# Weights first, four steps' inputs made on chip, the early convolution inside step 1, and another issuer for the stage stores

## The reference

```python
# x (B, T, D), cond (B, D)
# layer 0: depthwise causal convolution along T with K = 128 taps; cond is the tap matrix (tap, channel)
x = x + (conv_causal(x, cond[:, None, :]) + b)
# layer 1: a GRU over T, its first state is cond, then the residual
gi = x_t @ W_ih + b_ih ; gh = h @ W_hh + b_hh          # (B, 3D) each
r = sigmoid(i_r + h_r) ; z = sigmoid(i_z + h_z)
n = tanh(i_n + r * h_n) ; h = (1 - z) * n + z * h      # 64 steps, one after the other
out = x + all h
```

## Time and profile before

| | us |
|---|---|
| three runs, median | 1177.78 (1176.2 to 1178.16) |
| profiled execution, its own time | 1179.38 |
| its span | 1177.5 |
| TensorE busy | 1135.4 (96%) |
| VectorE busy | 690.0 (59%) |
| ScalarE busy | 506.3 (43%) |
| GpSimd busy | 145.7 (12%) |
| mean granted TensorE clock | 0.997 |

### The profile page before, as it was taken

One profiled execution on the slowest core, in us unless ns is written; L12 is line 12 of the kernel. 1 busy time (PEld: TensorE's weight loads), 2 busy tenths in 40 slices (PEclk: granted clock), 3 DMA queues, 4 the chain that ended last, 5 costly groups with the idle time before them and its releaser, 6 DMA issues.

```text
span 1177.5 us, 16672 instructions
## 1 busy us (share of the span) xinstructions
PE 1135.4 (96%) x5796; PEld 960.1 (82%) x5796; DVE 690.0 (59%) x1026; ACT 506.3 (43%) x965; POOL 145.7 (12%) x175
## 2 busy tenths in 40 slices
PE   1999999999999999999999999999999999999997
PEld 1977887878888888888888888888888888888885
DVE  2746775766775375555555655655555555655554
ACT  4527776767775343333323233333333333233332
POOL 0320010001001421111111000111111111100110
PEclk9999999999999999999999999999999999999999
DMA  9988888888863601110111111011111011111001
GB/s 247 286 193 167 160 172 165 173 174 171 174 151 91 147 18 37 36 35 25 31 36 36 36 36 28 25 36 36 36 36 27 27 36 36 36 36 32 26 23 27
DMA packets 284008, 96.97 MB, mean 82 GB/s; under 512 B 212688, under 2 KB 275664, under 8 KB 281920
## 3 DMA queue, kind: packets, MB, share of 16 engines
q1 hardware_dynamic: 278208, 91.83, 34.0%
q0 software_dynamic: 1664, 3.41, 0.9%
q10 hardware_dynamic: 4096, 1.22, 0.4%
HBM read 62.26 MB, written 34.14 MB: 82 GB/s over the span
## 4 chain that ended last, share of the span: by engine, by line
PE 92%; SPq 2%; ACT 1%; DMA 1%; DVE 1%; issue 1%; ACTq 0%; DVEq 0%
PE bank L1081 40%; PE sum_a L1140 17%; PE sum_c L1140 12%; PE bank L1174 7%; PE bank L1178 4%; PE sum_c L1081 3%; PE sum_a L1105 3%; PE bank L1043 2%; PE sum_a L1070 2%; PE sum_c L1105 1%; SPq L422 1%; PE sum_c L1070 1%; DMA early<-early_result 1%; SPq L435 1%; ACT toep_early L655 0%
## 5 line engine op out<-in xcount | busy, mean ns | idle before, releaser
L1081 PE MATMUL bank<-w_hh_hi,hT_hi 128*128 128x512 f32 x584 | 232.3, 398 | 0.1
L1081 PE MATMUL bank<-w_hh_lo,hT_hi 128*128 128x512 f32 x584 | 228.4, 391 | 0.0
L1081 PE MATMUL bank<-w_hh_hi,hT_lo 128*128 128x512 f32 x584 | 227.8, 390 | 0.0
L783 ACT ACTIVATE n_gate<-q 128x512 f32<-128x512 f32 x64 | 40.5, 633 | 249.2 <-DVE q L984 249.2
L1081 PEld LDWEIGHTS bank<-w_hh_hi,hT_lo 128*128 128x128 f32 x584 | 109.9, 188 | 23.9
L1081 PEld LDWEIGHTS bank<-w_hh_hi,hT_hi 128*128 128x128 f32 x584 | 109.9, 188 | 22.4 <-DVE hT_lo L838 0.5
L1081 PEld LDWEIGHTS bank<-w_hh_lo,hT_hi 128*128 128x128 f32 x584 | 110.3, 189 | 17.8
L823 ACT ACTIVATE hT_hi<-bank 128x512 fp32r<-128x512 f32 x63 | 37.6, 597 | 140.1 <-PE bank L1043 140.1
L838 DVE TENSOR_TENSOR hT_lo<-bank,hT_hi 128x512 fp32r<-128x512 f32 x64 | 44.1, 689 | 87.4 <-ACT hT_hi L823 87.0
L596 POOL TENSOR_TENSOR x_sum<-xT 128x256 f32<-128x256 f32 x23 | 17.3, 752 | 628.2 <-DMA xT<-xres 628.1
L889 DVE TENSOR_TENSOR x_parts<-x_unit,x_parts 128x512 fp32r<-128x512 f32 x64 | 70.5, 1102 | 39.0 <-ACT x_parts L706 38.8
(11 more groups left out here) (153 smaller groups left out, 2375.2 us busy)
## 6 DMA issues: line engine op xcount, KB each, us to landing
x_unit<-in_x_dram SPq DMA_DIRECT2D x64, 256.0 KB, 4.6
out_dram<-outZ SPq DMA_DIRECT2D x204, 64.0 KB, 1.6
toep_ring<-kernel_parts SPq DMA_DIRECT2D x128, 96.0 KB, 3.2
xres<-stage SPq DMA_DIRECT2D x32, 384.0 KB, 4.8
xT<-xres SPq DMA_DIRECT2D x192, 64.0 KB, 1.9
early<-early_result SPq DMA_DIRECT2D x4, 1024.0 KB, 13.6
xT<-early SPq DMA_DIRECT2D x60, 64.0 KB, 2.1
out_dram<-outZ POOLq DMA_DIRECT2D x52, 64.0 KB, 3.0
```

What stands on the lines that cost most here:

```text
L1081: mm = nc.tensor.matmul(psum[:, :], a[:, rows], b[w][:, cols], start=False, stop=stop and n == 2, skip_group_check=True)
```

## The change

- SP issues W_hh first, then W_ih; x_early comes after all the small tiles are used up, since these now lie in its place (from x_at on) and not in that of W_hh. The biases come as rows and are spread by a product with ones, and are kept by ScalarE.
- x1 of steps 0 to 3 (DIRECT) is made on chip: x's first four rows are loaded (x_rows), transposed, scaled and biased by ScalarE (y_base), and VectorE adds the lagged terms (y_sums).
- Step 0 multiplies h's and x's parts in the order in which the gates arrive (first_step_products).
- The early convolution is made in step 1, two banks at each of points 2 to 9, and stored through three tiles in place of four.
- The late convolution has 11 banks a step in steps 3 to 14 (POINTS = 12, of which 11 carry banks). FIRST_PAIR is 20. The combined blocks are made one step later.
- GpSimd issues the stage stores, between the outputs' stores.

```diff
-POINTS = 10
-BULK_FIRST, BULK_LAST = 1, 13
+POINTS = 12
+DIRECT = 4
+EARLY_STEP, EARLY_POINT = 1, 2
+BULK_FIRST, BULK_LAST = 3, 14
...
-    FIRST_PAIR = EARLY + 2
+    FIRST_PAIR = EARLY + 4
...
+        BULK_SLOTS = [(t, p) for t in range(BULK_FIRST, BULK_LAST + 1) for p in range(POINTS - 1)]
+        BULK_OF = {slot: m for m, slot in enumerate(BULK_SLOTS[:NBANK])}
...
+            load_weights(1, w_hh)
             load_weights(0, w_ih)
...
+            sp.wait_ge(toep_early_pool_ready, C0 // 2)
+            sp.wait_ge(toep_early_dve_ready, C0 // 2)
+            sp.wait_ge(y_base_ready, KB * DIRECT)
+            sp.wait_ge(y_sum_ready, Y_SUMS[-1])
+            for b4 in range(4):
...
+                ).then_inc(x_early_loaded, 16)
...
-                if m % 8 == 2 and m > 2:
-                    store_stage(m // 8 - 1)
...
+            for t in range(BULK_FIRST, BULK_LAST + 1):
+                for point in range(POINTS):
+                    m = bulk_bank(t, point)
+                    if m is not None and m % 8 == 2 and m > 2:
+                        store_stage(m // 8 - 1)
+                    if point == 1:
+                        store_early_out(t - 1)
+            store_stage(NBANK * 2 // STAGE - 1)
...
+            high_weights(1, R)
+            act.wait_ge(bias_early_done, 1)
...
+            high_weights(1, N)
+            act.wait_ge(conv_bias_loaded, 16 * (QUADS + 2))
+            y_base(0)
...
+            high_weights(1, Z)
+            y_base(1)
+            y_base(2)
+            high_weights(0, R)
+            y_base(3)
+            high_weights(0, N)
+            high_weights(0, Z)
...
+                act.wait_ge(gh_z_done, t + 1)
+                if not isinstance(i, bass.RuntimeValue) and t == 0:
+                    act.wait_ge(y_sum_ready, Y_SUMS[1])
+                    nc.scalar.activation(xT_hi[:, :], xT[1][:, :], ACT.Copy).then_inc(xT_hi_ready, 1)
...
+            for psum, rows, bias in ((ps_r, 2, b_rows[0:2, R:R + D]), (ps_z, 2, b_rows[0:2, Z:Z + D]),
+                                     (ps_in, 1, b_rows[0:1, N:NG]), (ps_hn, 1, b_hn_row[:, :])):
+                mm = nc.tensor.matmul(psum[:, :], ones[0:rows, :], bias, start=True, stop=True)
...
+            def first_step_products():
+                for psum, gate in ((ps_r, R), (ps_hn, N), (ps_z, Z)):
+                    for k in range(KB):
+                        low_weights_ready(1, k, gate)
+                        block_product(psum, hT_hi, hT_lo, 1, gate, k, False)
+                    if gate == R:
+                        pe.wait_ge(x_rows_loaded, 16 * KB)
...
+                for psum, gate, done in ((ps_r, R, gh_r_done), (ps_in, N, gh_n_done), (ps_z, Z, gh_z_done)):
+                    for k in range(KB):
+                        low_weights_ready(0, k, gate)
+                        mm = block_product(psum, xT_hi, xT_lo, 0, gate, k, k == KB - 1)
...
+                            for n in early_banks(t, g * POINTS // GROUPS):
+                                early_products(n)
                             bulk(bulk_bank(t, g * POINTS // GROUPS))
```

More of the change, by code:

```diff
@@ L136, in conv_residual_gru @@
     toep_early = place("toep_early", G0 * P)
[L137 to L140, removed]
+    result = [place(f"early_result{n}", G0 // RESULTS * B) for n in range(RESULT_TILES)]
+    assert top[0] <= outT_at
     top[0] = x_at
@@ L171, in conv_residual_gru @@
     lag0_row = place("lag0_row", 8, parts=EARLY)
[L172 to L175, removed]
+    h0 = place("h0", D)
+    ones = place("ones", P, parts=2)
+    b_hn_row = place("b_hn_row", D, parts=1)
+    assert top[0] <= toep_at
+    top[0] = bias_first_at
+    b_rows = place("b_rows", NG, parts=2)
+    assert top[0] <= bias_first_at + 2 * NCOL * KW
+    top[0] = outZ_at
+    tap_blocks = place("tap_blocks", EARLY * G0)
+    assert top[0] <= outZ_at + 2 * D * KW
     ctx = ExitStack()
@@ L494, in step @@
                     return
+                if isinstance(t, int) and t == BULK_LAST:
+                    for n in range(2):
+                        sp.wait_ge(stage_stored[n], 32 * (PAIRS // STAGE // 2))
+                    sp.wait_ge(outT_ready, BULK_LAST)
+                    for late in range(EARLY, BULK_LAST + RING):
+                        load_xT(late % RING, T - 1 - late)
                 sp.wait_ge(outZ_ready, t + 1)
@@ L498, in step @@
                     if t == BULK_LAST:
[L499 to L503 removed]
+                        load_xT(u, T - 1 - BULK_LAST - RING)
                         sp.wait_ge(x_lo_ready, NBLOCK)
@@ L767, in step @@
                 first_half(bulk_bank(t, 0))
-                if not isinstance(i, bass.RuntimeValue) and t == 0:
-                    for n in range(QUARTERS):
-                        act.wait_ge(early_stored[n], 16)
                 act.wait_ge(gh_r_done, t + 1)
@@ L945, in step @@
                     x_first_low(0, u + 1)
-                    for n in range(2, NCOMBO):
-                        combo_low(n)
                 if odd and follows:
@@ L993, in step @@
                     sums_low(slice(D, 2 * D), sum34_hi_ready, sum34_lo_ready, j + 1)
+                if not isinstance(i, bass.RuntimeValue) and t == 0:
+                    low_part(xT_lo, xT[1], xT_hi, xT_hi_ready, xT_lo_ready, 2)
+                split(split_block(t, 4))
+                second_half(bulk_bank(t, 4))
+                early_evicts(t, 4)
                 dve.wait_ge(h_less_n_ready, t + 1)
@@ L1052, in _, with transpose_x @@
+            mm.then_inc(banks_opened, 1)
+            def transpose_x(t):
+                for k in range(KB):
+                    mm = nc.tensor.transpose(ps_x[t][:, k * P:(k + 1) * P],
+                                             x_rows[:, k * D + t * P:k * D + (t + 1) * P], ident[:, :])
+                mm.then_inc(x_rows_done, 1)
             pe.wait_ge(hT_hi_ready, 1)
-            for psum in (ps_r, ps_z, ps_in, ps_hn):
-                mm = nc.tensor.matmul(psum[:, :], hT_hi[:, 0:P], hT_hi[:, :], start=True, stop=True)
```

430 lines of the change are left out of this document (239 added, 191 removed).

## The result

The change makes the kernel slower: 1216.56 us (1213.44 to 1218.12) against 1176.99, ratio 1.0334 [1.0309, 1.036]. The forecast was 1183.6: its sign is right, and 33 us are missing. The profiled execution took 1216.79, its span is 1214.6, 37.1 more than before.

What follows compares the result with a forecast made beforehand. TensorE, busy for 96% of the span, was taken as the bound. The terms -24.0, +28.0, +0.7, +1.6, -3.3 and +2.8 sum to +5.8 us, giving 1183.6; range 1172 to 1192, the forecast's own 1180 to 1188.

Steps and rivals of the forecast that it cites:

- 55.5 for step 0's transposes: Start: the transposes of h ending step 0 stand at 55.5 us, 24.0 earlier than 79.52.
- A start at 17: ScalarE's weight copies begin at 17 us; its last high block is written between 41 and 45.
- DMA bound: Start: six gates at 4.65 us plus lesser loads put the last gate at 42.9, or 32 if ACT's loads hide.
- The chain behind the last high block: Start: 5.8 us of ScalarE's step 0 work, then 5.4 of products; transposes 11 us after the last high block.
- The opening products: Start: new 32-bit bias products, 1.7 us apiece, 7 in all, at least 0.9 apiece, hidden under the weight load.
- The early convolution, +28.0 and 0.7 for switching: Step 1: the moved 64 products cost 28.0 us, and eight switches to 32-bit products and back 0.7.
- 28.0 was the convolution that is no longer ahead of them: Start: moving the convolution takes 28.0 us from before step 0's transposes; the start loses 4, leaving -24.0.
- -3.3 and +2.8: Late convolution's stage: its beginning gains 3.3 us; its middle loses 2.8, from +7 for late pairs and -4.2 for moved stores.
- Rival A: Stage: SP's queue was the limit, so moving its stores removes the middle's 8 us; 1170 or 1173; chance 0.22.
- Rival D: Stage: transfers, not issue, make pairs late, nothing given back; +7 in the middle, 1188; chance 0.44 together with the forecast.
- one pair fewer: Later steps: FIRST_PAIR from 18 to 20 replaces one 32.0 us pair by two direct steps of 33.6, +1.6.
- All four: Rival A, Rival D, B (quicker start, transposes at 51, 1179, chance 0.20) and C (DMA saturates in stage, 1196, 0.14).

Runs made afterwards that it cites:

- experiment 3: Changed kernel with x_rows as one load of whole rows and the kernel_parts stores issued behind ScalarE's last weight block; 1215.93 us, ratio 1.0309.
- Experiments 1 to 4: Changed kernel: 1, x_rows as one whole-row load, 1212.68 us; 2, W_ih issued only after x_rows landed, 1220.91; experiment 3 and experiment 4 have own lines.
- Numbers 10 to 12: Kernel before: 10, without the early convolution's 64 products, 1178.6 us; 11, also without step 1's DRAM trip, 1179.39; 12, without that trip alone, 1179.6.
- experiment 4: Experiment 3's kernel with W_ih issued only when tap_blocks has landed; 1202.15 us, ratio 1.0192.
- number 8: Kernel before with only the stage stores moved from SP to GpSimd; 1173.48 us, ratio 0.995.
- experiment 5: Changed kernel with GpSimd's four tap blocks made by ScalarE; 1224.94 us, ratio 1.0388.
- experiment 6: Experiment 4's kernel with GpSimd's four tap blocks made by ScalarE; 1201.41 us, ratio 1.0185.

## Why the prediction was wrong, step by step

**The step that failed is the one to 55.5 for step 0's transposes: "A start at 17"** for ScalarE's weight copies, and a path from there that runs over ScalarE alone. The transposes came at 83.15. The copies began at 42.57, 25.6 late. From there to the transposes the prediction had 38.5 us, and 40.6 passed; that is the other 2.1. That these two are close is luck: ScalarE was through 21.4 us after its start, where 27.5 were forecast, and the transposes followed 19.2 us after that in place of 11, because VectorE was behind. A right start would not have been enough either: in experiment 3 the copies begin at 17.93 and the transposes stand at 76.31. The prediction's two bounds for the start were a DMA bound (transfers) and a ScalarE bound (work). The time for which the issue of ScalarE's own loads is held, the item between them, was given no term, though the trace of before has x_early's four loads at 13.87 us of issue. Experiments 1 to 4 show that it isn't one load but the order of traffic: with both matrices queued by SP (handed over by 20.1), x_rows was held for 28.6 us and kernel_parts for 12.5, and tap_blocks landed late, 21.8 us from issue to use. Only when W_ih is held back as well do the transposes come to 61.0. What remains to 55.5 is VectorE's work, with pauses of 1.06 us at most from 23.5 to 50; its tap blocks and x's lagged terms had no sum in the prediction.

**The DMA bound.** "The last gate lands at 42.9" held as a bound: the weights had landed by 38. Without the 4 us for tap_blocks and kernel_parts, which were moved only after them (40 to 44), the sum gives 38.9. It was not what decided.

**The chain behind the last high block,** 11 us: its length is right, its beginning is not. It starts with VectorE's last low parts, at 72.6, and takes 10.5 from there; behind the last high block (63.9) it is 19.2.

**The opening products.** "1.7 us apiece, 7 in all", and at the least 0.9: four products took from 6.52 to 13.71, 7.2 us or 1.8 apiece, so the upper end was right. The page has two records for each. They hid under the wait that followed, as forecast.

**The early convolution, +28.0 and 0.7 for switching.** Step 1 took 45.03 us, where 45.5 was forecast: 16.8 + 28.0 + 0.2. The product count and the price were right, x_early's price of 0 too, though it was issued at 69.96 in place of 43.5, because step 0 was as late.

**"28.0 was the convolution that is no longer ahead of them."** Numbers 10 to 12 show that this credit stood on three legs. TensorE's stream (79.4), the trip of x1 through DRAM (79.5 to 80.4) and the wait for the stores (77.2) ended side by side, so the convolution sat in their shadow at its old place. The change takes away all three, and experiment 4 does have T0 18.5 us earlier than before; but every microsecond of it had to come from a faster start, while the work taken out of the shadow costs its whole 28.0 in step 1, where nothing hides it. By the prediction's other terms break-even needed T0 at 49.7 (79.5 - 28.2 - 1.6), by the measured ones at 46.1 (79.5 - 30.7 - 2.7), and the best order tried gave 61.0.

**The stage.** -3.3 and +2.8 put its loss at 12.3; with the switching 13.0 against 15.5 measured. Idle time before banks was forecast at 6 to 14 us, released by loads; after it is 8.7 us in five waits, 5.2 of them without a releaser in the profile and 3.5 behind `stage`, an eviction. That the stores on GpSimd give back 4.2 was too little: 4.8 us in number 8's stage and 5.7 in its time, some 7.5 here. Rival A's mechanism is thus at work in the middle, though 3.9 of its 8 us of stalls remain in number 8 (steps 2 to 13), and the reason against it ("an issue time of 4.78 us is back-pressure") was not one. Rival D, nothing given back, is refuted by number 8, and with it the use that was made of the Trainium skill ("DMA: Bandwidth & Descriptors", Issuing engines are not separate DMA queues): that another issuer saves only the time to issue is no reason to expect nothing, where that time stands in SP's program, in order, ahead of loads that TensorE waits for.

**The end,** 0, and one pair fewer, +1.6: measured +2.7 together.

**The rivals.** All four rest on a start of 51 to 57, so none could hold. The range lacked a rival for the start: one in which loading and preparing don't overlap. 42.9 for the last transfer and then 38.5 would have given T0 at 81 and a time near 1209.

## What to carry to other kernels

Before an edit puts the weights first, list every DMA that stands behind them on any queue, and every instruction that stands behind those in its engine's program: here three sets of lesser transfers, 0.5 to 1 MB each, in turn held ScalarE or VectorE for 12 to 29 us. Price work at its old place by taking it out and running; a stream that is busy to the end can still be covered by two other limits that end with it. And when stores and loads share one in-order issuer, try the stores elsewhere by themselves first: that one edit is the only part of this change that a run by itself shows to pay.

## What the runs showed of the hardware

- An issue can be held for long while the engine behind it idles: 28.56 us for four loads of 256 KB in small pieces, 8.12 for one store, with weights queued; the same store took 0.76 when they had landed (40.29 in the changed kernel). Small pieces alone cost issue time too: x_early's four loads took 11.74 us with no weights queued.
- How long a load takes goes by what is queued at its issue: tap_blocks, 512 KB, 21.8 us behind both matrices, some 6.1 behind one (issued 17.40, used at 23.51).
- GpSimd needs 4.3 to 5.2 us for a 128x1024 TENSOR_SCALAR; ScalarE makes the same block in 1.97 to 2.1 (experiments 5 and 6). VectorE's own took 1856 ns in the mean in the changed kernel, and still 1658 with GpSimd's gone (experiment 5); in experiment 6 the shortest took 1.12. What else slows them wasn't found.
- The four opening bias products of 512 columns in 32 bits took 7.2 us together, 1.8 each, in two records each; the GRU's products in fp32r go at 0.227.
- A wait of TensorE can cost more than it lasts: behind the one of 3.64 us the granted clock was 0.50 in 212 to 214, and the step took 5.4 us more than one without a wait.
